# A two-layer cross-attention kernel on one core: first-layer norms as one operation per tile, norm weights applied on leaving PSUM

## The chip, the cores and the metric

The kernel runs on one core of a Trainium2 chip. A core has five engines, each with its own instruction queue: TensorE (PE, matrix products), VectorE (DVE), ScalarE (ACT), GpSimd (POOL) and SyncE (SP, which here only starts transfers). They meet through semaphores. The metric is the device time of one execution in microseconds; less is better.

## What is computed

Two cross-attention layers over 2 batches of 512 tokens of width 256, with a context of 1024 rows of width 192. Layer 0 (which the program counts as −1, and which the change touches) has one head, layer norms on both inputs, and biases:

```python
qn = _layer_norm(q_feat, g_q, be_q)          # (x - mu) * rsqrt(var + EPS) * gamma + beta
kvn = _layer_norm(kv_feat, g_kv, be_kv)
q = einsum('bnq,eq->bne', qn, Wq) + bq
k = einsum('bmk,ek->bme', kvn, Wk) + bk
v = einsum('bmk,ek->bme', kvn, Wv) + bv
attn = softmax(einsum('bne,bme->bnm', q, k), axis=-1)
x = q_feat + einsum('bnf,ef->bne', einsum('bnm,bme->bnf', attn, v), Wd) + bd
...
# layer 1: 8 heads of 256, keys and values from the raw context, mask; out = LayerNorm(ctx @ Wo + x)
```

## The kernel before

Every fp32 operand of a large product is split into a rounded high part and a low remainder, and a product is made of three passes (`three`, line 569) or of five for scores and values. ACT writes the high parts (`round_...`), DVE or POOL the low parts (`split_...`). Wq and Wk, and Wv and Wd, are first multiplied with each other (`absorb`), so that queries meet the normalised context directly. The weights come through two buffers, `ring`, as pieces.

The order of each engine's work is written out by hand, in one long list per engine: SP lines 325 to 422, POOL 426 to 564, PE 568 to 980, ACT 984 to 1332, DVE 1336 to 1789. An instruction that waits holds everything behind it on its engine.

Layer 0 in the order of PE (lines 788 to 867): a product of spread biases with the weights (792); transposes of the normalised tokens, chunks 0 and 1 (`turn_chunk`, `xn`); weight products (`absorb`); small bias products (803); transposes of the normalised context, chunks 2 to 5 (`kvn`); `queries` for batch 0; then `scores(-1, j)` for blocks of 128 queries, j = 0 to 3, each into the same two PSUM banks `ps_scores`, which DVE's `minimum` (1352) must have read before the next block may write. ACT's `exp`, PE's `turn_probs`, ACT's `round_probs` and DVE's `split_probs` follow for each block, and `values` for the batch; batch 1's norms run between these.

A norm takes, for one tile: statistics and moments on DVE (`ln_stats`, `ln_moments`), a power of −1/2 on POOL (`rsqrt`), centring and the weight on DVE (`ln_centre`), scaling on ACT (`scale_tiles`), the bias on POOL (`bias_tiles`); for half of the context tiles scaling and bias are one operation on DVE (`ln_scale_context`). Every score is shifted by a query-dependent number, which DVE sums from the normalised tokens (`sum_shift`, `finish_shift`) ahead of the first minimum of a batch.

## Time and profile before

| | us |
|---|---|
| median of 3 runs | 501.74 (501.72 to 502.06) |
| profiled execution | 501.67 |
| its span, first to last instruction | 499.70 |
| PE busy in the span | 474.2 |
| DVE / ACT / POOL busy | 332.2 / 291.6 / 245.4 |

The span is what the trace covers; the profiled execution's own time is 1.97 us longer. A row of the timeline gives start, duration, engine, line, operation, output and inputs, the number of merged instructions (x4), and in brackets how long the engine was idle before it and what released it. PE's ends are modelled: two rows that follow each other overlap by their latency, so the time of one in a sequence is read from start to start. A product of plain fp32 operands shows as two instructions.

### The profile page before, as it was taken

What the parts mean: (1) busy time and instruction counts of PE and PEld (TensorE: products, weight loads), DVE (VectorE), ACT (ScalarE), POOL (GpSimd) and SP (SyncE); (2) the same over time, 40 slices, a digit from 0 to 9 for tenths busy, and PEclk for the clock granted to TensorE, in tenths of its full rate; (3) what the DMA queues carried; (4) which work ended last, traced back from release to release, by engine and by line L of the source; (5) the groups of instructions that cost most, each with busy time, mean ns of one, the idle gap of its engine ahead of it and who ended that gap; (6) DMA issues with size and microseconds to landing.
All of it is one profiled execution on the core that took longest, in us unless ns stands there. A gap on an engine that the chain in (4) does not pass through costs nothing.

```text
span 499.7 us, 7565 instructions
## 1 busy us (share of the span) xinstructions
PE 474.2 (95%) x2424; PEld 395.8 (79%) x2424; DVE 332.2 (66%) x679; ACT 291.6 (58%) x482; POOL 245.4 (49%) x153
## 2 busy tenths in 40 slices
PE   0999999999999999999999999999999999999994
PEld 0877787787878888888888888888888888888893
DVE  4999866476685657565856585658565765673666
ACT  4667476467664756566666665656565655556332
POOL 4636763555855353637272717172727263454004
PEclk9999999999999999999999999999999999999998
DMA  8413013667765565665656564647473746562002
GB/s 263 147 45 127 1 29 120 212 206 227 246 214 182 177 202 176 205 211 168 210 168 210 168 214 164 226 153 238 140 244 135 252 137 220 168 210 64 0 2 84
DMA packets 53975, 81.97 MB, mean 164 GB/s; under 512 B 5793, under 2 KB 43073, under 8 KB 53825
## 3 DMA queue, kind: packets, MB, share of 16 engines
q1 hardware_dynamic: 44992, 50.16, 33.8%
q10 hardware_dynamic: 8960, 31.54, 16.8%
q8 instruction: 11, 0.18, 0.2%
q14 instruction: 12, 0.09, 0.1%
HBM read 49.16 MB, written 32.51 MB: 163 GB/s over the span
## 4 chain that ended last, share of the span: by engine, by line
PE 74%; DVE 8%; DMA 7%; ACT 4%; issue 3%; POOL 2%; SPq 1%; DVEq 0%; POOLq 0%; ACTq 0%
PE ps_scores L626 27%; PE ps_o L658 6%; PE ps_o L651 5%; PE ps_o L650 5%; PE ps_o L657 5%; PE ps_o L652 5%; DMA scratch<-probs 3%; PE ps_task L574 2%; PE ps_task L573 2%; PE ps_task L572 2%; DMA probs_t_lo<-scratch 2%; DMA ring<-in_weights_a 2%; PE ps_out L572 2%; PE ps_out L573 1%; PE ps_out L574 1%
## 5 line engine op out<-in xcount | busy, mean ns | idle before, releaser
L514 POOL TENSOR_TENSOR probs_t_lo<-probs_t_lo,probs_t_hi 128x1024 fp32r<-128x1024 f32 (+1 forms) x75 | 146.5, 1967 | 177.5 <-ACT probs_t_hi L1018 177.4
L1018 ACT ACTIVATE probs_t_hi<-probs_t_lo 128x1024 fp32r<-128x1024 f32 (+1 forms) x75 | 64.7, 881 | 37.2 <-DMA probs_t_lo<-scratch 34.7
L626 PE MATMUL ps_scores<-key_hi,q_hi 128*128 128x512 f32 x144 | 57.8, 402 | 1.3 <-DVE neg_scores L1352 0.8
L1339 DVE RECIPROCAL row_inv<-row_sum 128x1 f32<-128x1 f32 x72 | 11.3, 159 | 70.4 <-PE ps_scores L626 68.4
L650 PE MATMUL ps_o<-probs_t_hi,val_hi 128*128 128x512 f32 (+1 forms) x144 | 56.7, 393 | 1.1 <-issue 0.9
L626 PE MATMUL ps_scores<-key_rem,q_lo 128*128 128x512 f32 x144 | 56.6, 393 | 0.5 <-DVE q_lo L1434 0.3
L626 PE MATMUL ps_scores<-key_rem,q_hi 128*128 128x512 f32 x144 | 56.6, 393 | 0.0
L626 PE MATMUL ps_scores<-key_lo,q_hi 128*128 128x512 f32 x144 | 56.6, 393 | 0.0
L626 PE MATMUL ps_scores<-key_hi,q_lo 128*128 128x512 f32 x144 | 56.4, 392 | 0.0
L651 PE MATMUL ps_o<-probs_t_lo,val_hi 128*128 128x512 f32 (+1 forms) x144 | 56.3, 391 | 0.0
L658 PE MATMUL ps_o<-probs_t_lo,val_rem 128*128 128x512 f32 (+1 forms) x144 | 56.2, 392 | 0.0
L657 PE MATMUL ps_o<-probs_t_hi,val_rem 128*128 128x512 f32 (+1 forms) x144 | 55.8, 389 | 0.0
L652 PE MATMUL ps_o<-probs_t_hi,val_lo 128*128 128x512 f32 (+1 forms) x144 | 55.6, 386 | 0.0
L1376 DVE STREAM_TRANSPOSE probs<-probs 128x1024 f32<-128x1024 f32 x30 | 37.4, 1246 | 25.0 <-ACT probs L1006 24.8
L1376 DVE STREAM_TRANSPOSE neg_scores<-neg_scores 128x1024 f32<-128x1024 f32 x30 | 37.3, 1242 | 15.1 <-ACT neg_scores L1006 15.1
L444 POOL TENSOR_TENSOR w_lo<-ring,w_hi 128x1024 fp32r<-128x1024 f32 x17 | 40.9, 2408 | 6.2 <-ACT w_hi L1098 6.2
L1006 ACT ACTIVATE neg_scores<-neg_scores,row_min 128x1024 f32<-128x1024 f32 x30 | 34.5, 1148 | 13.1 <-DVE row_min L1369 13.1
L1369 DVE CUSTOM_DVE_ANT_0 probs<-ps_scores,mask_bias 128x1024 f32<-128x1024 f32 x32 | 38.9, 1216 | 3.2 <-PE ps_scores L626 3.2
L1006 ACT ACTIVATE probs<-probs,row_min 128x1024 f32<-128x1024 f32 x30 | 34.5, 1151 | 11.1 <-DVE row_min L1369 11.0
L1369 DVE CUSTOM_DVE_ANT_0 neg_scores<-ps_scores,mask_bias 128x1024 f32<-128x1024 f32 x32 | 38.8, 1213 | 0.6 <-issue 0.6
L626 PEld LDWEIGHTS ps_scores<-key_hi,q_hi 128*128 128x128 f32 x144 | 27.0, 188 | 7.5 <-DVE neg_scores L1352 2.2
L626 PEld LDWEIGHTS ps_scores<-key_rem,q_lo 128*128 128x128 f32 x144 | 27.0, 188 | 7.2 <-DVE q_lo L1434 0.6
(256 smaller groups left out, 1097.5 us busy)
## 6 DMA issues: line engine op xcount, KB each, us to landing
probs_t_lo<-scratch SPq DMA_DIRECT2D x240, 128.0 KB, 2.9
scratch<-neg_scores ACTq DMA_DIRECT2D x30, 512.0 KB, 3.1
scratch<-probs ACTq DMA_DIRECT2D x30, 512.0 KB, 3.7
ring<-in_weights_a SPq DMA_DIRECT2D x9, 512.0 KB, 5.2
ring<-in_weights_b SPq DMA_DIRECT2D x9, 512.0 KB, 5.1
ring<-in_keys_t SPq DMA_DIRECT2D x4, 512.0 KB, 3.2
ctx_raw<-in_context SPq DMA_DIRECT2D x2, 768.0 KB, 9.5
ring<-in_context SPq DMA_DIRECT2D x16, 96.0 KB, 2.6
```

Of the source, the lines that this page charges most:

```text
L444: nc.gpsimd.tensor_tensor(w_lo[:, :], ring[r][:, :], w_hi[:, :].bitcast(f32), ALU.subtract)\
L514: nc.gpsimd.tensor_tensor(pt_lo[b][:, t, k, :], pt_lo[b][:, t, k, :].bitcast(f32), moved_part(j, k).bitcast(f32), ALU.subtract).then_inc(m ...
L626: last = pe.matmul(ps_scores[:, n], left, right[:, n], start=(i == 0), stop=(i == len(passes) - 1))
L650: pe.matmul(o0, val_hi[b][:, kt, :], hi, start=(kt == 0), stop=False)
L651: pe.matmul(l0, val_hi[b][:, kt, :], lo, start=False, stop=False)
L652: pe.matmul(o0, val_lo[b][:, kt, :], hi, start=False, stop=(kt == KT - 1))
L657: pe.matmul(o1, val_rem[b][:, kt, :], hi, start=(kt == 0), stop=False)
L658: last = pe.matmul(l1, val_rem[b][:, kt, :], lo, start=False, stop=(kt == KT - 1))
L1006: act.activation(dst, src, ACT.Exp, bias=row_min[:, j:j + 1], scale=-1.0, accum_out=row_sum[:, j:j + 1]).then_inc(exped, 1)
L1018: act.activation(moved_part(j, k), pt_lo[b][:, t, k, :].bitcast(f32), ACT.Copy)\
L1369: dve.tensor_tensor_reduce(out=tiles[j % 2][:, :], in0=ps_scores[:, :], in1=mask_bias[:, b, :], scale=1.0, scalar=BIG, op0=ALU.add, op1=AL ...
L1376: dve.transpose(tiles[j % 2][:, :], tiles[j % 2][:, :]).then_inc(blocks_turned, 1)
```

## The change

One norm operation per tile: ACT makes (x · r − m · r) from the raw tile for tokens and half of the context (`norm_tokens`, `norm_context` on ACT), DVE makes (x − m) · r for the other context tiles (`norm_context` on DVE). For ACT's form DVE first makes −m · r (`shift_means`), which needs POOL's r. The norm weights are multiplied in when ACT and DVE take transposed chunks (`round_chunk`, `split_chunk`) and the output weights (`round_b`, `split_b0`) out of PSUM; for that the weights come as one row on one partition (`gain_row`) and PE turns them into columns (`gains`). The norm biases are folded into the projection biases by reductions over the weights (`fold_bias`). The score shift is made on PE, from a split vector of two columns and the split tokens (`sum_shift`), kept by ACT (`keep_shift`), turned back by PE (`turn_shift`) and finished on DVE. PE multiplies the identity with itself 20 times ahead of the first chunks and 8 times ahead of the weight products (`keep_running`); nothing reads the result. Tokens, context rows and outputs are assigned to partitions in stretches that lie together in memory. Transfers, and the second weight piece's rounding on ACT, change places. The core of the diff (the lines not shown are declarations, the same edits for the context and the outputs, and `split_w` and `fold_bias`, which follow below it):

```diff
-    x_tiles = x.rearrange("(t p) d -> p t d", p=P)
+    x_tiles = x.rearrange("(b p t) d -> b p t d", p=P, t=QT)
...
 @block.sync
+            sp.dma_start(resid[:, 0:QT, :], x_tiles[0]).then_inc(x_loaded[0], 16)
+            sp.dma_start(ctx_raw[:, 0:CTX_HALF, :], ctx_tiles[0, :, 0:CTX_HALF, :]).then_inc(ctx_loaded[0], 16)
+            sp.dma_start(ctx_raw[:, CTX_HALF:KT, :], ctx_tiles[0, :, CTX_HALF:KT, :]).then_inc(ctx_loaded[1], 16)
             sp.dma_start(ring[0][:, :], weights_a[0]).then_inc(ring_loaded[0], 16)
+            sp.dma_start(be_row[:, :], rows_q[1].partition_broadcast(P)).then_inc(be_row_loaded, 16)
+            sp.dma_start(kv_row[:, :], rows_kv[1].partition_broadcast(P)).then_inc(kv_row_loaded, 16)
             sp.dma_start(ring[1][:, :], weights_b[0]).then_inc(ring_loaded[1], 16)
...
 @block.tensor
-                    pe.wait_ge(task_free, T_VEC + 1)
+                    pe.wait_ge(chunk_split, 1)
...
+            def keep_running(count):
+                for i in range(count):
+                    pe.matmul(ps_scores[:, BANK:BANK + P], ident[:, :], ident[:, :], start=True, stop=True)
+            def sum_shift(b, bank):
+                for k in range(DT):
+                    mv = slice(b * QUERIES, (b + 1) * QUERIES)
+                    pe.matmul(bank[0:2, :], w_pair[:, k, :], xt_hi[:, k, mv], start=(k == 0), stop=False)
+                    last = pe.matmul(bank[0:2, :], w_pair[:, k, :], xt_lo[:, k, mv], start=False, stop=(k == DT - 1))
+                last.then_inc(shift_rowed, 1)
+            def turn_shift(b, bank):
+                pe.wait_ge(shift_kept, b + 1)
+                if b == 0:
+                    for k in range(DT):
+                        pe.matmul(bank[:, V_CONST:V_CONST + 1], ones[:, :], shift_parts[:, k:k + 1],
+                                  start=(k == 0), stop=(k == DT - 1))
+                for t in range(QT):
+                    last = pe.transpose(bank[:, 2 * t:2 * t + 2], shift_rows[:, t, :], ident[0:2, 0:2])
+                last.then_inc(shift_turned, 1)
...
-            pe.wait_ge(spread_made, DT)
-            pe.wait_ge(ring_loaded[0], 16)
-            raw = ring[0]
-            for k in range(DT):
-                pe.matmul(vec_bank[:, DIM:2 * DIM], spread[:, k, :], raw[:, k * DIM:(k + 1) * DIM],
-                          start=(k == 0), stop=(k == DT - 1))
             pe.wait_ge(ident_loaded, 16)
-            for c in range(X_CHUNKS):
+            pe.wait_ge(gain_row_loaded, 48)
+            for n in range(N_GAINS):
+                last = pe.transpose(vec_bank[:, V_GAINS + n:V_GAINS + n + 1], gain_row[:, n * P:(n + 1) * P],
+                                    ident[0:1, 0:1])
+            last.then_inc(gains_turned, 1)
+            keep_running(20)
+            for c in range(X_CHUNKS + 1):
                 turn_chunk(0, c)
+            keep_running(8)
             pe.wait_ge(piece_split, PC_A0 + 1)
             absorb(T_A0, 0)
             absorb(T_A0b, 1)
+            for c in range(X_CHUNKS + 1, CHUNKS):
+                turn_chunk(0, c)
+            pe.wait_ge(bias_folded, 2)
...
-            for c in range(X_CHUNKS, CHUNKS):
-                turn_chunk(0, c)
             pe.wait_ge(chunk_split, X_CHUNKS)
+            pe.wait_ge(w_split, 1)
+            sum_shift(0, w_bank)
             pe.wait_ge(task_free, T_VEC + 1)
             queries(T_Q0, 0, 0)
             queries(T_Q0b, 0, 1)
-            pe.wait_ge(chunk_split, CHUNKS)
+            turn_shift(0, w_bank)
+            pe.wait_ge(chunk_split, CHUNKS - 2)
...
             for c in range(QT):
                 values(-1, 0, c)
+                if c == 0:
+                    pe.wait_ge(task_free, T_Q1 + 1)
+                    sum_shift(1, ps_task)
+                if c == 1:
+                    turn_shift(1, ps_task)
...
 @block.scalar
+            act.dma_start(ident[:, :], identity).then_inc(ident_loaded, 16)
+            act.dma_start(gain_row[:, 0:DIM], rows_q[0:1]).then_inc(gain_row_loaded, 16)
+            act.dma_start(gain_row[:, DIM:DIM + CTX], rows_kv[0:1]).then_inc(gain_row_loaded, 16)
+            act.dma_start(gain_row[:, DIM + CTX:2 * DIM], rows_kv[0:1, P:CTX]).then_inc(gain_row_loaded, 16)
             act.dma_start(cols[:, :], vectors).then_inc(cols_loaded, 16)
-            act.dma_start(ident[:, :], identity).then_inc(ident_loaded, 16)
...
+            def norm_tokens(b):
+                act.wait_ge(means_made, 2 * b + 1)
+                for t in range(KT, LN_TILES):
+                    n, x_tile = b * LN_TILES + t, b * QT + t - KT
+                    act.activation(xn[:, x_tile, :], resid[:, x_tile, :], ACT.Identity,
+                                   scale=rstd[:, n:n + 1], bias=neg_means[:, n:n + 1]).then_inc(x_normed, 1)
...
-                act.activation(dst, chunk_bank(b, c)[:, 0:BANK], ACT.Copy).then_inc(chunk_rounded, 1)
+                act.activation(dst, chunk_bank(b, c)[:, 0:BANK], ACT.Copy, scale=scale).then_inc(chunk_rounded, 1)
...
-            round_weights(16, 1)
+            keep_shift(0, w_bank)
             act.wait_ge(vec_made, 1)
             round_queries(T_Q0, 0, 0, 0)
             round_queries(T_Q0b, 0, 1, 0)
+            round_weights(16, 1)
+            act.wait_ge(bias_v_folded, 1)
+            for k in range(DT):
+                act.activation(spread[:, DT + k, :], ones[:, :], ACT.Copy, scale=bias_cols[:, C_BV + k:C_BV + k + 1])\
+                    .then_inc(spread_made, 1)
             exp(-1, 0)
...
 @block.vector
+            def norm_context(b):
+                dve.wait_ge(rstd_made, 3 * b + 3)
+                for t in range(CTX_HALF, KT):
+                    n = b * LN_TILES + t
+                    dve.tensor_scalar(kvn[b][:, t, 0:CTX], ctx_raw[:, b * KT + t, :], moments[:, n, 0:1],
+                                      rstd[:, n:n + 1], ALU.subtract, ALU.mult).then_inc(ctx_normed[1], 1)
+            def shift_means(b, first, end, rstds):
+                n = slice(b * LN_TILES + first, b * LN_TILES + end)
+                dve.wait_ge(rstd_made, 3 * b + rstds)
+                dve.scalar_tensor_tensor(neg_means[:, n], moments[:, n, 0], -1.0, rstd[:, n], ALU.mult, ALU.mult)\
+                    .then_inc(means_made, 1)
...
             ln_stats(0, x_token_tiles, x_loaded[0])
             ln_moments(0, KT, LN_TILES)
-            dve.wait_ge(q_rows_loaded, 16)
-            ln_centre(0, x_token_tiles)
-            ln_stats(0, range(KT), ctx_loaded[0])
-            ln_moments(0, 0, KT)
+            ln_stats(0, range(CTX_HALF), ctx_loaded[0])
+            ln_moments(0, 0, CTX_HALF)
+            shift_means(0, KT, LN_TILES, 1)
+            shift_means(0, 0, CTX_HALF, 2)
...
+            ln_stats(0, range(CTX_HALF, KT), ctx_loaded[1])
+            ln_moments(0, CTX_HALF, KT)
+            norm_context(0)
             dve.wait_ge(piece_hi, HI_OF[PC_A0])
...
             split_queries(T_Q0, 0, 0, 0)
             split_queries(T_Q0b, 0, 1, 0)
-            sum_shift(0, range(QT))
-            finish_shift(0)
+            split_chunk(0, 4)
+            split_chunk(0, 5)
+            finish_shift(0, w_bank[:, 0:2 * QT])
+            dve.wait_ge(ring_loaded[1], 16)
+            fold_bias(C_BV, ring[1], 0, kv_row, bias_v_folded)
             minimum(-1, 0, 0)
             ln_stats(1, x_token_tiles, x_loaded[1])
             ln_moments(1, KT, LN_TILES)
+            shift_means(1, KT, LN_TILES, 1)
             split_b0(T_B0, 0)
             split_b0(T_B0b, 1)
```

```python
def fold_bias(side, raw, first, row, folded_by):
    for k in range(DT):
        dve.tensor_tensor_reduce(out=probs[...], in0=raw[...], in1=row[:, :], op0=ALU.mult, op1=ALU.add,
                                 accum_out=bias_parts[:, side + k:side + k + 1]).then_inc(bias_summed, 1)
    dve.wait_ge(bias_summed, side + DT)
    dve.tensor_tensor(bias_cols[:, n], bias_parts[:, n], cols[:, n], ALU.add).then_inc(folded_by, 1)
def split_w():
    dve.tensor_copy(w_pair[:, :, 0], made).then_inc(w_hi_made, 1)
    dve.tensor_tensor(shift_parts[:, 0:DT], bias_cols[...], bias_cols[...], ALU.mult)
    dve.wait_ge(w_hi_made, 1)
    dve.tensor_tensor(w_pair[:, :, 1], made, w_pair[:, :, 0], ALU.subtract).then_inc(w_split, 1)
```

## Rows read from the trace of the kernel before

**Rows 1.** The page's first part: engines, busy us, share of the span, instructions.

```profile
PE 474.2 (95%) x2424; PEld 395.8 (79%) x2424; DVE 332.2 (66%) x679; ACT 291.6 (58%) x482; POOL 245.4 (49%) x153
```

**Rows 2.** Stretches: length; PE, PEld, DVE, ACT, POOL busy us; granted clock; DMA share; GB/s.

```profile
33.00:46.80 13.80, 11.94 (x65) 9.27 (x65) 12.96 (x33) 12.39 (x23) 8.81 (x7) 1.00 0.41 153
46.80:59.05 12.25, 11.76 (x56) 8.98 (x56) 12.04 (x34) 4.89 (x12) 10.94 (x13) 1.00 0.00 1
...
200.00:249.00 49.00, 49.00 (x245) 41.22 (x244) 31.83 (x60) 29.70 (x46) 24.25 (x12) 1.00 0.62 201
```

**Rows 3.** Timeline of the head, DVE, POOL and ACT, 4 to 14 us.

```profile
4.72 1.41 DVE L1470 BATCH_NORM_STATS2 stats<-resid 128x6 f32<-128x256 f32 x4 [4.72 <-DMA resid<-in_x]
...
6.77 1.02 POOL L431 TENSOR_TENSOR rstd<-var_eps,minus_half 128x4 f32<-128x4 f32 x1 [4.63 <-DVE var_eps L1481]
...
7.82 1.71 ACT L1127 ACTIVATE xn<-xn,rstd 128x256 f32<-128x256 f32 x4 [1.16 <-POOL rstd L431]
...
9.84 2.17 DVE L1470 BATCH_NORM_STATS2 stats<-ctx_raw 128x6 f32<-128x192 f32 x8 [1.15 <-DMA ctx_raw<-in_context]
11.65 1.06 ACT L1098 ACTIVATE w_hi<-ring 128x1024 fp32r<-128x1024 f32 x1 [2.12 <-DMA ring<-in_weights_a]
...
12.74 1.23 DVE L1556 TENSOR_TENSOR w_lo<-ring,w_hi 128x1024 fp32r<-128x1024 f32 x1
```

**Rows 4.** Timeline of PE alone, 11 to 40 us.

```profile
11.76 2.04 PE L792 MATMUL ps_o<-ring,b_full 128*128 128x256 f32 x4 [11.76 <-DMA ring<-in_weights_a]
13.60 1.91 PE L779 MATMUL ps_turn<-ident,xn 128*128 128x128 f32 x8
...
16.59 0.41 PE L572 MATMUL ps_out<-w_hi 128*128 128x256 f32 x1
...
16.99 0.28 PE L574 MATMUL ps_out<-w_hi,w_lo 128*128 128x256 f32 x1
...
17.46 0.95 PE L803 MATMUL ps_o<-cols,ring 128*128 128x1 f32 x8
...
23.53 0.39 PE L574 MATMUL ps_task<-xt_hi,a_lo 128*128 128x512 f32 x1
...
31.84 1.03 PE L827 MATMUL ps_out<-ring,b_full 128*128 128x256 f32 x4
...
39.52 1.04 PE L779 MATMUL ps_o<-ident,xn 128*128 128x128 f32 x8
```

**Rows 5.** Timeline of all engines from the last query products to the third score block.

```profile
22.95 2.39 POOL L444 TENSOR_TENSOR w_lo<-ring,w_hi 128x1024 fp32r<-128x1024 f32 x1 [2.93 <-ACT w_hi L1098]
...
24.68 0.74 DVE L1434 SCALAR_TENSOR_TENSOR q_lo<-ps_task,vec,q_hi 64x512 fp32r<-64x512 f32 x1 [0.36 <-ACT q_hi L1075]
...
27.20 1.28 DVE L1352 TENSOR_SCALAR_CACHE_REDUCE neg_scores<-ps_scores,neg_shift 128x1024 f32<-128x1024 f32 x1
...
28.54 0.50 PE L626 MATMUL ps_scores<-key_hi,q_hi 128*128 128x512 f32 x1
...
30.37 1.02 POOL L431 TENSOR_TENSOR rstd<-var_eps,minus_half 128x4 f32<-128x4 f32 x1 [5.03 <-DVE var_eps L1481]
...
31.67 1.28 DVE L1352 TENSOR_SCALAR_CACHE_REDUCE neg_scores<-ps_scores,neg_shift 128x1024 f32<-128x1024 f32 x1
...
33.02 0.50 PE L626 MATMUL ps_scores<-key_hi,q_hi 128*128 128x512 f32 x1 [0.16 <-DVE neg_scores L1352]
```

**Rows 6.** DMA issues of the first 30 us: KB each, us from issue to landing.

```profile
cols<-in_vectors ACTq DMA_DIRECT2D x1, 3.0 KB, 3.3
mask_bias<-in_mask ACTq DMA_DIRECT2D x1, 8.0 KB, 6.9
```

**Rows 7.** DVE's groups by line and shape, 27.2 to 59.05 us: busy us, mean ns.

```profile
L1501 DVE SCALAR_TENSOR_TENSOR kvn<-kvn,rstd,kv_rows 128x192 f32<-128x192 f32 x4 | 3.0, 799 | 0.0
L1492 DVE SCALAR_TENSOR_TENSOR kvn<-ctx_raw,moments,kv_rows 128x192 f32<-128x192 f32 x8 | 2.7, 412 | 0.0
...
L1529 DVE CUSTOM_DVE_ANT_0 ctx_raw<-xn,rem_sum 128x256 f32<-128x256 f32 x4 | 1.4, 409 | 0.0
```

More of the change, by code:

```diff
@@ L415, in store @@
                 sp.wait_ge(fin_made[half], count)
[L416 removed]
+                sp.dma_start(out_tiles[b, :, t, :], tiles[:, t, :])\
                     .then_inc(stored, 16)
@@ L623, in scores @@
                                 pe.wait_ge(task_free, task + (1 if i == 2 else 2))
+                        if late_keys is not None and half == 1 and i in (0, 3):
+                            pe.wait_ge(chunk_split, late_keys + (1 if i == 0 else 2))
                         if keys is not None and i == 3 and half == 0:
@@ new lines, in shift_means @@
+            def shift_means(b, first, end, rstds):
[4 more added lines that the diff above has]
+            def fold_bias(side, raw, first, row, folded_by):
+                n = slice(side, side + DT)
+                width = row.shape[1]
+                for k in range(DT):
+                    spare, src = side % (2 * DT) * DIM + k * width, first + k * DIM
+                    dve.tensor_tensor_reduce(
+                        out=probs[:, spare:spare + width], in0=raw[:, src:src + width], in1=row[:, :], scale=1.0, scalar=0.0, op0=ALU.mult, op1=ALU.add,
+                        accum_out=bias_parts[:, side + k:side + k + 1]).then_inc(bias_summed, 1)
+                dve.wait_ge(bias_summed, side + DT)
+                dve.tensor_tensor(bias_cols[:, n], bias_parts[:, n], cols[:, n], ALU.add).then_inc(folded_by, 1)
```

248 lines of the change are left out of this document (127 added, 121 removed).

## Prediction

> **What bounds the kernel now.** I read the page's busy shares first: TensorE (PE) is busy 95% of the span, no other engine above 79% [rows 1]. Then the stretches: from 200 to 249 us, which stands for the long middle, PE is busy 49.00 of 49.00 us, so nothing that shortens another engine's work there can shorten the kernel; the change touches nothing there. Its edits all lie before about 60 us, and there PE has holes: 13.80 − 11.94 = 1.86 us in 33.0 to 46.8, 12.25 − 11.76 = 0.49 us in 46.8 to 59.05 [rows 2]. VectorE (DVE) is busy 12.96 of 13.80 and 12.04 of 12.25 us in the last two, so it, in a chain with PE and ScalarE (ACT), ends those holes. Third, the timeline of the head: PE does nothing before 11.76 us, when the first weights land [rows 4]. So a delay or a gain that stands on PE at 60 us is carried to the end unchanged, and the task is to find where PE stands there. The sum is made against the profiled execution, 501.67 us (span 499.70 and 1.97 around it); the median of three is 501.74, the same within 0.07.
>
> I use two marks of before. T is the end of the first query products: the last starts at 23.53 and is followed 0.23 us later, so T = 23.76 [rows 4]. The second mark is the start of the third score block, 33.02 [rows 5].
>
> **Part 1, the head up to T.** Removed: the two 256-column products with spread biases (11.76 to 13.60, the start of the first transposes, 1.84 us), GpSimd's (POOL) bias additions, DVE's centring. Added on PE: four tiny transposes of the gains, 20 idle products, 8 more, two extra bias products, four products for the score shift.
>
> When PE starts: it now waits for the identity and three gain rows on ACT's queue. The third gain row is issued after three others, at about 0.73 + 3 × 0.5 = 2.2 us. The biases, first on that queue, took 3.3 us to land, the mask, third, 6.9 [rows 6]; so the start is 5.5 us by the one and 9.1 by the other, and not before the tokens that move at the same time, 4.7 [rows 3]. I take 5.5: the queue's big transfer, the identity, now goes first and beside the tokens. The Trainium skill (DMA: Bandwidth & Descriptors, "Queues, rings and completion order") says that an engine serves the queues in turn, packet by packet, and in "Anatomy of one DMA" it puts the fixed cost near 2 us; by that the start would be an estimated 4.2 us, the low part of the weights would decide, and the sum would be 504.7. The mask's 6.9 us speaks against it, the biases' 3.3 us for it in part.
>
> An idle product is 128 columns of fp32 and issues two instructions. The two 256-column products at 11.76 make four instructions in 1.84 us, so a 128-column one costs 0.46 us at that clock; the same pair at 31.84 takes 1.03, so a half-size one about 0.23 to 0.26 [rows 4]. The clock: 256-column instructions last 0.41 us at 16.59 and 0.28 at 16.99, the step from 1.2 to 2.4 GHz, 5.1 us after PE began. If PE begins at 5.5, the step comes at 10.6. Gains to 6.1; ten idle products to 10.6 at 0.45; ten more at 0.23 to 12.9; twelve transposes (eight take 1.04 at 39.52 including the last one's tail, so 0.115 each) to 14.3; eight idle products to 16.1. The idle products keep PE warm, but the last ones stand in its queue ahead of the weight products.
>
> Are the inputs there by 16.1? Tokens land at 4.72, their reciprocal deviation is ready at 6.77 + 1.02 = 7.79 [rows 3]. From token landing to the first weights (11.65), 1.77 MB came in 6.9 us; at that rate half the context lands at 6.3, all of it at 7.8 and the weights, with 0.45 MB fewer ahead, at 9.9. Statistics of four context tiles (2.17 / 8 each) and moments end at 8.2, POOL's power at 9.3, DVE's mean shift, which waits for it, at 9.6; behind that wait stand the second half's statistics, which then end at 11.3, POOL at 12.4, four normalising operations (at most the 2.7 / 8 of a centring each [rows 7]) at 13.8, the weights' low part (1.23) at 15.0. ACT normalises tokens 8.4 to 10.1 (1.71), four context tiles to 11.6, rounds the weights (1.06) to 12.7. So the low part is ready at 15.0, against 13.97 before, and PE's own queue at 16.1 decides. Weight products: twelve at 0.12 (16.99 to 17.46 holds four) end at 17.5, where before they ended at 17.46. The whole gain in clock is spent on idle products.
>
> From there to T before: 6.3 us. After: twelve transposes, 1.4; sixteen bias instructions at 0.95 / 8, 1.9; then PE waits for DVE to copy, split and subtract the small vector (three short operations, 0.15 to 0.2 each: 0.6); four shift products at 0.23, 0.9; twelve query products, 2.8. T comes at 25.1, **1.3 us later**. Ends: +0.5 with a start at 4.7, +4.9 with 9.1 (every us of start is a us of T, until the low part at 15.0 decides).
>
> **Part 2, T to the third score block.** Two queues grow. ACT now rounds the second weight piece after both query halves (T + 0.8 to T + 1.9), and POOL splits it in 2.39 [rows 5]: T + 4.35, then twelve products, and the second score block starts at T + 5.8; before it was 28.54 = T + 4.8. DVE, after the second query split (24.68 + 0.74 = T + 1.66), has two more key splits (0.7 each), the shift's finish (three short ones, 0.5) and the value-bias fold (two reductions of about 0.35 and an addition, 0.8; the removed reductions took 0.41 each [rows 7]), so the first minimum starts at T + 4.4 instead of T + 3.44: **+0.95**. ACT's first exponential also waits for that fold, but the minimum is later.
>
> Then the wait that the change adds: after batch 1's token moments DVE's mean shift waits for POOL's power of the variances just made. Row 30.37 has this power at 1.02 us [rows 5]; with two hand-overs and the operation itself 1.3 us. Behind it on DVE stand the two output-weight splits, the mask steps and the second minimum. Before, minimum to minimum was 31.67 − 27.20 = 4.47; now 5.8, so the second starts at T + 10.2 against T + 7.91: **+2.25 in all**, the 0.95 included. The third score block needs the bank that this minimum empties, and starts that much later. PE's second block ends near T + 8.2 and cannot hide it.
>
> **Part 3, to 59 us.** DVE loses the token centring ahead of the third minimum, 2.7 and 3.0 us of context work and 1.4 of shift sums [rows 7], some 7 us; it gains about 2 us of new work. What is that worth? At most the 1.86 us of holes. But scores and minimum alternate on one pair of banks: after the lift the third minimum waits for its scores instead of the centring. I take 0.35 us of the 1.86 (bounds 0.3 and 1.9), since ACT's order between the third block and the value products is unchanged. In batch 1 PE gets four shift products (0.9) and four transposes (0.5) between value products; the 0.49 us of holes there go. **+0.9.** ACT waits for the shift rows ahead of four context tiles, 3 us before PE asks for these. The plain-scale multiplications on leaving PSUM cost nothing more on ACT, and up to 0.06 us each on DVE, hidden. Contiguous memory: at most 0.3 us of the last store, taken as 0.
>
> **Sum:** 1.3 + 2.25 − 0.35 + 0.9 = +4.1, so 501.67 + 4.1 = 505.8 us.
>
> **Rivals.** First, *faster by DVE's relief*: DVE is the engine without pause after 33 us, and about 7 us go. If POOL's power is out of the way when DVE needs it and the extra operations before the minima fit beside PE, then all holes go (−2.49), the shift costs 1.4, the head is even (start 4.7 and low part at 14.5), the store gives 0.2: 500.4. It decides if the second minimum starts by T + 8. For it: DVE's 12.96 of 13.80; against it: program order, which puts the wait ahead of the minimum. Chance 0.13.
>
> Second, *about even*: the clock steps up early, or the head is 1.3 us shorter than I have it (T at 23.8) and the power trip costs half: 0 + 1.6 − 1.5 + 0.9 = +1.0, 502.7 or a little below. Chance 0.14.
>
> Third, *gain rows late*: PE starts at 9.1, T + 4.9, total 509.4. For it: the mask's 6.9 us; against: what lay ahead of the mask. Chance 0.08.
>
> That the change does not do what it says: the idle products may not lift the clock before the weight products (they are 128 columns, as the transposes in before are): then the 28 cost 12.6 us instead of 8.6 and T is 4 us later still, near 510; this lies within the third's chance.
>
> **How the numbers follow.** My forecast has 0.65: 503.5 (start 4.7, holes worth 1.9) to 507.5 (start 7.2). The range takes in the even case and most of the way to the late one, and leaves out the faster case and the end of the late one, 0.19 in all: 501.5 to 508.5. Faster and slower mean by over 0.2% (1.0 us), about what a measurement of this kernel can tell from no change: faster 0.13, same 0.14, slower 0.73.
>
> **What would show it.** Right: PE idle products from about 5.5 to 13 and eight more ending near 16; first 0.28 us weight product at once; T near 25; a DVE idle of about 1.2 us put down to POOL's power between first and second minimum; third score block at 36.5 to 37.5; 200 to 249 unchanged. Wrong: a start of PE before 4.5 or after 8; weight products before 14.5 (then the inputs were earlier than I have them); the second minimum within 8 us of T; PE's holes from 33 to 47 gone.

## The result, and the profile after

The changed kernel takes 508.58 us (median of 4, 508.48 to 508.86), the kernel before beside it 501.90: a ratio of 1.0135, 95% interval 1.0119 to 1.0151. The forecast was 505.8, range 501.5 to 508.5: the direction was right, the size too small, and the time lies just outside the range. The profiled execution took 508.56, of which 506.4 are the span. Two single executions in the experiments, 792.49 us (the kernel before with the added wait) and 1228.55 us (the kernel with six edits, in the execution that was profiled), are left out of every median here.

The page of the changed kernel, engines as in [rows 1]:

```profile
PE 484.6 (96%) x2504; PEld 405.2 (80%) x2504; DVE 326.5 (64%) x666; ACT 295.8 (58%) x483; POOL 231.9 (46%) x139
```

PE has 10.4 us more work, mostly idle products; DVE and POOL have 5.7 and 13.5 us less. From 200 to 249 us (columns as in [rows 2]) PE is busy 49.00 of 49.00 us in both kernels, so what was lost was lost early:

```profile
200.00:249.00 49.00, 49.00 (x246) 41.19 (x245) 31.84 (x59) 29.78 (x47) 24.26 (x12) 1.00 0.59 193
```

The timeline of PE in the head, to be held against [rows 4]:

```profile
6.47 0.56 PE L829 MATMUL ps_o<-ident,neg_scores 1*128 1x1 f32 x4 [6.47 <-DMA neg_scores<-in_rows_kv]
6.95 6.97 PE L799 MATMUL ps_scores<-ident 128*128 128x128 f32 x40
13.76 1.04 PE L793 MATMUL ps_turn<-ident,xn 128*128 128x128 f32 x8
...
15.07 1.95 PE L799 MATMUL ps_scores<-ident 128*128 128x128 f32 x16
16.78 0.36 PE L584 MATMUL ps_task<-w_hi 128*128 128x256 f32 x1
...
19.60 0.95 PE L847 MATMUL ps_o<-bias_cols,ring 128*128 128x1 f32 x8
20.41 1.03 PE L851 MATMUL ps_o<-bias_cols,ring 128*128 128x1 f32 x8
22.05 0.59 PE L805 MATMUL ps_turn<-xt_hi,w_pair 128*2 128x512 f32 x1 [0.61 <-DVE w_pair L1594]
22.43 0.63 PE L806 MATMUL ps_turn<-xt_lo,w_pair 128*2 128x512 f32 x1
22.86 0.63 PE L805 MATMUL ps_turn<-xt_hi,w_pair 128*2 128x512 f32 x1
...
27.01 0.40 PE L586 MATMUL ps_task<-xt_hi,a_lo 128*128 128x512 f32 x1
```

The last query product starts at 27.01 and is followed 0.24 us later, so T is 27.25 against 23.76. The shift products at 22.43 and 22.86 are 0.43 us apart, those around 27 us 0.23. The stretches of the same profile say why (length; PE, PEld, DVE, ACT, POOL busy; granted clock; DMA share; GB/s):

```profile
19.60:22.05 2.45, 1.84 (x19) 1.79 (x17) 0.57 (x5) 1.17 (x3) 0.00 (x0) 0.97 0.00 0
22.05:25.00 2.95, 2.95 (x8) 1.65 (x9) 1.28 (x2) 0.59 (x1) 0.00 (x0) 0.50 0.55 178
25.00:27.25 2.25, 2.25 (x11) 1.83 (x10) 0.41 (x1) 0.69 (x1) 0.00 (x0) 0.92 0.00 0
```

PE did 1.84 us of one-column products, then waited 0.61 us for DVE; from there the granted clock is 0.50, the lower level (1.2 GHz), for about 3 us. Sixteen products took 27.25 − 22.05 = 5.20 us; at 0.23 each they take 3.7. The fall costs 1.5 us.

From T to the third score block, all engines, against [rows 5]:

```profile
29.16 2.38 POOL L460 TENSOR_TENSOR w_lo<-ring,w_hi 128x1024 fp32r<-128x1024 f32 x1 [17.28 <-ACT w_hi L1157]
...
30.86 0.90 DVE L1582 CUSTOM_DVE_ANT_0 probs<-ring,kv_row 128x192 f32<-128x192 f32 x1
...
32.19 1.28 DVE L1429 TENSOR_SCALAR_CACHE_REDUCE neg_scores<-ps_scores,neg_shift 128x1024 f32<-128x1024 f32 x1
...
35.36 1.01 POOL L455 TENSOR_TENSOR rstd<-var_eps,minus_half 128x4 f32<-128x4 f32 x1 [3.82 <-DVE var_eps L1559]
36.40 0.16 DVE L1573 SCALAR_TENSOR_TENSOR neg_means<-moments,rstd 128x4 f32<-128x4 f32 x1 [1.12 <-POOL rstd L455]
...
38.08 1.28 DVE L1429 TENSOR_SCALAR_CACHE_REDUCE neg_scores<-ps_scores,neg_shift 128x1024 f32<-128x1024 f32 x1
...
39.43 0.50 PE L640 MATMUL ps_scores<-key_hi,q_hi 128*128 128x512 f32 x1 [1.28 <-DVE neg_scores L1429]
```

The first minimum starts at T + 4.94 (before T + 3.44), the second at T + 10.83 (T + 7.91), the third block at T + 12.18 (T + 9.26): 2.92 us later against T, and the added wait stands there as forecast, 1.12 us of DVE's idle time put down to POOL's power. From the third to the fourth block both kernels take 4.08 us. Then the stretch from the fourth to the fifth block, first before, then after:

```profile
37.10:59.05 21.95, 20.26 (x102) 15.53 (x102) 20.89 (x56) 13.24 (x27) 17.50 (x17) 1.00 0.19 73
```

```profile
43.51:66.72 23.21, 21.44 (x111) 16.20 (x111) 18.03 (x43) 14.93 (x28) 13.67 (x13) 1.00 0.19 69
```

It is 1.26 us longer: PE has 1.18 us more work, and its idle time is 1.69 us before and 1.77 after, though DVE has 2.86 us less to do. At the fifth block the changed kernel is 3.49 + 2.92 + 1.26 = 7.67 us behind. From about 165 to 196 us it gets 0.93 back: there the profiled execution before has small waits for DVE (the largest, 0.41 us, at 195.43) and the changed one none:

```profile
195.43 0.38 PE L572 MATMUL ps_out<-b_hi,o_hi 128*128 128x256 f32 x1 [0.41 <-DVE b_lo L1448]
```

With that, 6.7 us arrive at the end of the span.

### The profile page after: what moved, and what is told of

It reads as the page before. It is cut to its first block, busy times and chain, and to the rows that moved or that the text cites. A ratio compares the mean times of both kernels' runs of the same rounds, so it can differ in the third digit from the quotient of the medians.

```text
span 506.4 us, 7697 instructions
## 1 busy us (share of the span) xinstructions
PE 484.6 (96%) x2504; PEld 405.2 (80%) x2504; DVE 326.5 (64%) x666; ACT 295.8 (58%) x483; POOL 231.9 (46%) x139
## 3 DMA queue, kind: packets, MB, share of 16 engines
q10 hardware_dynamic: 8966, 31.54, 16.5%
## 4 chain that ended last, share of the span: by engine, by line
PE 86%; DVE 5%; ACT 4%; issue 1%; POOL 1%; DMA 1%; ACTq 0%; DVEq 0%; POOLq 0%
PE ps_scores L640 29%; PE ps_o L664 7%; PE ps_o L672 7%; PE ps_o L665 7%; PE ps_o L671 6%; PE ps_o L666 6%; PE ps_task L586 3%; PE ps_task L585 3%; PE ps_task L584 3%; PE ps_out L584 2%; PE ps_scores L799 2%; PE ps_out L585 2%; PE ps_out L586 2%; PE ps_out L758 1%; PE ps_out L757 1%
## 5 line engine op out<-in xcount | busy, mean ns | idle before, releaser
L640 PEld LDWEIGHTS ps_scores<-key_rem,q_hi 128*128 128x128 f32 x144 | 27.0, 188 | 6.8 <-ACT q_hi L1132 0.4
```

The source lines that it names most:

```text
L640: last = pe.matmul(ps_scores[:, n], left, right[:, n], start=(i == 0), stop=(i == len(passes) - 1))
```

## Experiments

Times are medians; the kernel before took 501.3 to 501.8 beside them, and "less" and "more" are against the changed kernel's 508.58 unless another is named. T is always the end of the first query products.

**Why the clock fell.** First, the bias products ahead of chunks 3 to 5, so that the transposes cover DVE's split:

```diff
-            for c in range(X_CHUNKS + 1, CHUNKS):
-                turn_chunk(0, c)
             pe.wait_ge(bias_folded, 2)
...
             last.then_inc(task_done, 1)
+            for c in range(X_CHUNKS + 1, CHUNKS):
+                turn_chunk(0, c)
             pe.wait_ge(chunk_split, X_CHUNKS)
```

> The changed kernel with its 16 one-column bias products ahead of the transposes of chunks 3 to 5 instead of behind them; nothing left out. In the changed kernel PE waits 0.61 us for VectorE's split of the small vector, the granted clock falls from 0.97 to 0.50 and the next eight products are 0.42 us apart instead of 0.23. Theory (the one-column products directly followed by the wait let the clock fall): the transposes cover the split, the wait goes, the clock stays up, the first query products end 2.1 us earlier (0.6 wait, 1.5 clock) and so does everything behind them: 506.4, or 507 if some of it is given back between 165 and 196 us. Rival (the one-column products alone let the clock fall, whatever stands behind them): the transposes then run at half clock, 1.3 us longer, only the wait goes; 508 to 508.5.

505.78 us, 2.80 less. T is 24.43: 0.6 of the gain is the wait, 1.5 the clock, and 0.57 comes from the head, where the weight products started at 16.21 in this execution. PE's timeline: no wait, and products at the upper clock (0.24 us apart from the second on).

```profile
18.54 1.03 PE L848 MATMUL ps_o<-bias_cols,ring 128*128 128x1 f32 x8
...
20.70 0.47 PE L805 MATMUL ps_turn<-xt_hi,w_pair 128*2 128x512 f32 x1
21.01 0.40 PE L806 MATMUL ps_turn<-xt_lo,w_pair 128*2 128x512 f32 x1
21.25 0.39 PE L805 MATMUL ps_turn<-xt_hi,w_pair 128*2 128x512 f32 x1
```

The one-column products alone do not bring the clock down. Second, the changed kernel's own order with the wait filled:

```diff
+            pe.wait_ge(task_free, T_VEC)
+            for i in range(3):
+                pe.matmul(ps_out[:, 0:P], ident[:, :], ident[:, :], start=True, stop=True)
             pe.wait_ge(chunk_split, X_CHUNKS)
```

> The changed kernel, in its own order, with three idle products (0.7 us at full clock) put into the 0.61-us wait between the one-column bias products and the shift products; nothing left out. This tells the two causes of the fallen clock apart that the run with the bias products first couldn't. Theory (the wait behind the one-column products brings the clock down): with the wait filled the granted clock stays at its upper level, the shift and query products are 0.23 us apart, the first query products end 1.4 to 1.5 us sooner; 507.1. Rival (the 1.8 us of one-column products bring it down alone): the products behind are still 0.42 us apart, the idle ones also slow; 508.6 to 509.4.

506.84 us, 1.74 less, though no useful work was moved. The stretches of the idle products and of the sixteen products behind them:

```profile
20.82:21.56 0.74, 0.74 (x8) 0.74 (x8) 0.56 (x5) 0.00 (x0) 0.00 (x0) 1.00 0.00 0
21.56:25.24 3.68, 3.68 (x18) 2.70 (x17) 1.67 (x3) 1.28 (x2) 0.00 (x0) 1.00 0.39 142
```

Sixteen products in 3.68 us at a granted clock of 1.00, against 5.20: filling 0.6 us of waiting gives 1.5 us back. (T is 25.24, 2.01 sooner; the other 0.48 is again the head, where the weight products started at 16.30.) In all eight executions of these two runs the mean granted clock of the whole span is 0.995 or 0.996; in the four of the changed kernel it is 0.993 or 0.994.

**The idle products.** The eight behind the first transposes left out:

```diff
-            keep_running(8)
```

> The changed kernel without the eight idle products between the first transposes and the weight products; nothing left out. In the changed kernel those eight end at 16.78 us and the low part of the weights is there at 14.30. Theory (they stand in the queue ahead of work that is ready): the weight products start at 15.1 at full clock, the first query products end 1.6 to 1.7 us sooner, the clock still falls behind the one-column products; 506.9 to 507.2. Rival (the eight keep the clock up for the weight products): these start 0.21 us apart, end 0.6 us sooner at most; 508 or above.

506.41 us, 2.17 less. The weight products start at 15.16 instead of 16.78: the eight were only in the way. The profiled execution (505.32 us, the fastest of the four) shows one thing more: the wait is there, and the clock stayed up.

```profile
20.44 0.40 PE L805 MATMUL ps_turn<-xt_hi,w_pair 128*2 128x512 f32 x1 [0.61 <-DVE w_pair L1593]
20.68 0.39 PE L806 MATMUL ps_turn<-xt_lo,w_pair 128*2 128x512 f32 x1
```

So one-column products and a wait of 0.6 us do not always lose the clock. Of the seven profiles with this wait four show the fall (the changed kernel, without idle products, mean shift late, the queues; 5.19 to 5.27 us for the sixteen products) and three don't (without the eight, start early, batch 1's shift moved; 3.66 to 3.69); of the five without the wait none does (3.64 to 3.73). Within one kernel it shows in the times: with the mean shift moved (below), 505.55 us where the mean granted clock was 0.996, and 507.48 to 507.73 where it was 0.992. The Trainium skill (TensorE: Matmul & The Clock Gate, "What's actually happening") says of the step upward that "it's run-variable"; these runs show the same of the fall. What no run here tells is whether a wait of 0.6 us behind full-width products would lose the clock too; in the kernel before with an added wait (below) PE waits 1.00 us for POOL behind transposes, and the 512-column products behind it are 0.23 us apart, the distance of the upper clock.

PE started early, with twelve idle products on the tile of ones ahead of the wait for the gain rows:

```diff
+            pe.wait_ge(ones_set, 1)
+            for i in range(12):
+                pe.matmul(ps_scores[:, BANK:BANK + P], ones[:, :], ones[:, :], start=True, stop=True)
             pe.wait_ge(ident_loaded, 16)
```

> The changed kernel with 12 more idle products, on the tile of ones, ahead of its wait for the identity and the gain rows, so that PE runs from about 1 us instead of 6.47; nothing left out. This prices the step of the prediction that had PE start at 5.5 us and counted a microsecond of start as a microsecond of the first query products. Theory: the clock steps up near 6 us, the 20 idle products take 4.6 us instead of 6.8, the first transposes end near 13, the eight idle ones near 14.9, the weight products start near 15.0 instead of 16.78 and all that follows comes 1.7 us sooner: 506.8, with the clock falling as before behind the one-column products. Rival (the start doesn't count, the inputs of the transposes or the weights' low part hold PE): under 0.5 us, 508.1 or above.

504.64 us, 3.94 less. The 20 idle products take 4.6 us, and the weight products start 2.47 us sooner, now at the moment at which their low part is ready:

```profile
6.40 4.73 PE L799 MATMUL ps_scores<-ident 128*128 128x128 f32 x40
...
14.31 0.39 PE L584 MATMUL ps_task<-w_hi 128*128 128x256 f32 x1
```

The clock stayed up here as well (T at 23.30), which is the rest of the 3.94. What PE gets rid of ahead of the weight products counts one for one, as the prediction had it, until their low part decides. But it is the idle products that got shorter (6.8 us in the changed kernel): the gain rows landed at 6.09 here, and no run moves their landing by itself. Without any idle products:

```diff
-            keep_running(20)
...
-            keep_running(8)
```

> The changed kernel without its 28 idle products; nothing that is computed is left out. In the changed kernel the weight products start at 16.78 us at full clock (0.12 us apart), though the low part of the weights is ready at 14.30, so the idle products cost 2.4 us of waiting and buy the clock. Theory (the idle products pay for themselves): without them the weight products start at 14.3 but at half clock, twelve at 0.21 us end near 16.9 instead of 18.3, and the 12 transposes, 16 one-column products, 4 shift products and 12 query products that follow also run at half clock, so that the first query products end at 28 to 29 us instead of 27.25: 509 to 510.5 us in all. Rival (idle products are only a delay): the clock is up soon after the first weight product, the first query products end 2 us earlier and the time is 506 to 507.

509.23 us (508.73 to 509.58), 0.65 more, but not as expected: T is at 26.37, 0.9 sooner. PE runs only the first twelve transposes (10.16 to 13.0), waits 1.34 us for the low part of the weights, and the weight products are 0.21 us apart, the distance of the lower clock:

```profile
14.38 0.58 PE L584 MATMUL ps_task<-w_hi 128*128 128x256 f32 x1 [1.34 <-DVE w_lo L1646]
14.76 0.41 PE L585 MATMUL ps_task<-w_lo,w_hi 128*128 128x256 f32 x1
14.97 0.41 PE L586 MATMUL ps_task<-w_hi,w_lo 128*128 128x256 f32 x1
```

(The column of the granted clock reads 1.00 from 14.38 to 17.11 all the same; the kernel before reads 1.00 from 14 to 16 us too, where its products of 256 columns are 0.21 us apart. In the head the level has to be read from the distances.) The 0.9 us and more are lost again later: near 88 us PE waits 1.84 us for ACT (0.75 in the changed kernel), which had waited 0.97 for a transfer, and near 225 us 0.72 for DVE. Neither account fits: in the head of this kernel the idle products cost 0.9 us more than they bring, and why the kernel without them waits more later stays open.

**The two minima.** The mean shift behind the second minimum instead of ahead of it:

```diff
-            shift_means(1, KT, LN_TILES, 1)
...
             minimum(-1, 1, 0)
+            shift_means(1, KT, LN_TILES, 1)
```

> The changed kernel with VectorE's mean shift of batch 1's tokens moved from ahead of the second minimum to behind it; nothing left out. There VectorE idles 1.12 us on GpSimd's power of the variances. Theory (the wait stands on the chain): the second minimum starts 1.2 to 1.3 us sooner, the third score block too, and the time is 507.3 (507.8 if part is given back at 165 to 196 us). Rival (the bank is not what the third block waits for, or ScalarE behind the minimum sets the pace): the third block keeps its place and the time stays within 0.3 us of 508.6.

507.57 us, 1.01 less; T is 27.70, and the third block starts at T + 11.06, 1.12 sooner. The wait was on the chain.

```profile
38.76 0.50 PE L640 MATMUL ps_scores<-key_hi,q_hi 128*128 128x512 f32 x1 [0.46 <-DVE neg_scores L1429]
```

And the wait alone, put into the kernel before:

```diff
             ln_moments(1, KT, LN_TILES)
+            dve.wait_ge(rstd_made, 3)
```

> The kernel before with one wait added and nothing else: behind batch 1's token moments VectorE waits until GpSimd's power of these variances is done, as the changed kernel's mean shift makes it. This prices by itself the wait that the prediction put at 1.3 us. Theory: the moments end near 30.4 us, the power at 31.4, the output-weight splits, the mask steps and the second minimum start 1.1 to 1.3 us later, the third score block too: 502.4 to 502.7 against 501.3. Rival (the second minimum waits for its scores or for ScalarE anyway): not over 0.3 us, 501.6.

502.43 us (median of nine), a ratio of 1.0021 to the kernel before (1.0007 to 1.0036), 1.1 us more. T is 23.95, and the third block starts at T + 10.50, 1.24 later than in the kernel before:

```profile
31.62 0.42 DVE L1423 TENSOR_TENSOR b_lo<-ps_out,b_hi 128x256 fp32r<-128x256 f32 x1 [1.13 <-POOL rstd L431]
...
33.10 1.28 DVE L1352 TENSOR_SCALAR_CACHE_REDUCE neg_scores<-ps_scores,neg_shift 128x1024 f32<-128x1024 f32 x1
...
34.45 0.50 PE L626 MATMUL ps_scores<-key_hi,q_hi 128*128 128x512 f32 x1 [1.22 <-DVE neg_scores L1352]
```

Up to the third block the wait costs 1.24 us where it is added and gives 1.12 where it is taken out. Then the two queues, ACT's step first, DVE's two behind it:

```diff
+            round_weights(16, 1)
             keep_shift(0, w_bank)
...
             round_queries(T_Q0b, 0, 1, 0)
-            round_weights(16, 1)
...
+            dve.wait_ge(ring_loaded[1], 16)
+            fold_bias(C_BV, ring[1], 0, kv_row, bias_v_folded)
             dve.wait_ge(task_done, T_VEC + 1)
...
+            split_chunk(0, 4)
+            split_chunk(0, 5)
             split_queries(T_Q0, 0, 0, 0)
             split_queries(T_Q0b, 0, 1, 0)
-            split_chunk(0, 4)
-            split_chunk(0, 5)
             finish_shift(0, w_bank[:, 0:2 * QT])
-            dve.wait_ge(ring_loaded[1], 16)
-            fold_bias(C_BV, ring[1], 0, kv_row, bias_v_folded)
```

> The changed kernel with the order of three steps altered on their engines, nothing left out: ScalarE rounds the second weight piece ahead of keeping the shift, where it idles 3.2 us, instead of behind both query halves; VectorE folds the value biases ahead of its wait for the small vector, where it idles 2.2 us; and it splits the last two key chunks ahead of the query halves, where it idles 3.5 us. Theory (the two queues behind the first query products delay the first minimum and the second score block): the second score block starts 0.5 us sooner against the first, the first minimum 2 to 2.4 us sooner, the third block 1.5 to 2 us sooner; the time is 506.6 to 507.1, or 0.5 above that if part is given back later. Rival (PE's own order of work sets the third block): not over 0.5 us, 508.1 or above.

506.88 us, 1.70 less. The second block follows the first by 4.00 us (5.53 in the changed kernel), the first minimum starts at T + 3.41, where it waits for scores, and the third block 1.54 us sooner against T. (What each of the three moves gives alone was not run.) The fold's first reduction takes 0.35 us at its new place:

```profile
18.71 0.35 DVE L1582 CUSTOM_DVE_ANT_0 probs<-ring,kv_row 128x192 f32<-128x192 f32 x1
...
30.11 1.28 DVE L1429 TENSOR_SCALAR_CACHE_REDUCE neg_scores<-ps_scores,neg_shift 128x1024 f32<-128x1024 f32 x1 [1.29 <-PE ps_scores L640]
```

**Batch 1.** The four shift products moved behind the first query half, into a bank that is free there (ACT's `keep_shift` moves with them):

```diff
             queries(T_Q1, 1, 0, chunks=True)
+            sum_shift(1, ps_o[0])
...
+            pe.wait_ge(shift_kept, 2)
...
-                    sum_shift(1, ps_task)
```

> The changed kernel with batch 1's four shift products moved to where PE idles 0.51 us on VectorE, in a bank that is free there, and nothing else; nothing left out. This prices the shift of batch 1 alone, where the changed kernel's third to fourth stage is 1.26 us longer. Theory (four products of 0.23 and the transposes, 1.2 us of PE's time, and no relief from VectorE): of 0.9 us of products 0.4 to 0.6 go into the idle time; 508.0 to 508.2. Rival (VectorE's and ScalarE's normalising of the context makes that stage longer, not the products): no change, 508.5 or more.

506.19 us (505.73 to 508.85). The clock did not fall in the profiled execution (T at 25.48), so the total can't be compared; the stage can:

```profile
41.77:64.63 22.86, 21.38 (x110) 16.18 (x110) 17.93 (x43) 14.74 (x28) 13.66 (x13) 1.00 0.18 70
```

22.86 against 23.21: 0.35 of the 0.9 us of products went into idle time. What is left of the longer stage is PE's own added work: 21.38 us against 20.26 before, with 1.48 idle against 1.69. The one execution of the four at 508.85 us has a mean granted clock of 0.991, as where the clock falls, and shows no gain over 508.58; so the 0.35 us is shown in the stage and not in the total.

**All together.** The four diffs above in one: the bias products first, the mean shift late, the queues, and no eight idle products:

> The changed kernel with four edits together: bias products ahead of the transposes, mean shift behind the second minimum, three steps moved into idle time of ScalarE and VectorE, and no eight idle products; nothing left out. Alone the first three gave 2.8, 1.0 and 1.7 us. Theory (these losses lie one behind the other on one chain): they add, with 1.6 for the eight idle products, to 7.1 us, and the time is 501.5, level with the kernel before; what stays lost is 1.3 us in batch 1, what is gained is the relief of VectorE. Rival (they hide one another, or a later transfer sets the pace once the head is short): 503 to 504.5.

501.64 us, ratio to the kernel before 1.0006 (0.9996 to 1.0016): the four gains nearly add up, 6.94 us together where the single ones sum to 7.68, and T is at 23.06, ahead of before. This profile also tells what the relief of DVE is worth once the wait is gone: the third block starts at 32.61 (33.02 before), the fourth 4.09 us later (4.08 before), and the stretch from the fourth to the fifth is as long as in the changed kernel, with 1.70 us idle on PE:

```profile
36.70:59.87 23.17, 21.47 (x111) 16.20 (x111) 18.05 (x43) 14.95 (x28) 13.66 (x13) 1.00 0.18 69
```

With batch 1's shift products moved as above, and the mask steps ahead of the first minimum:

```diff
+            dve.wait_ge(mask_loaded, 16)
+            dve.tensor_scalar(mask_small, mask_small.bitcast(i32), 0.0, BIG, ALU.is_equal, ALU.mult)...
+            dve.tensor_scalar(mask_small, mask_small, 10.0, None, ALU.mult)...
             minimum(-1, 0, 0)
```

> The kernel of the four edits (501.64 us) with two more; nothing left out. The mask steps stand ahead of the first minimum, where VectorE idles 1.3 us on scores, instead of ahead of the second; batch 1's four shift products stand between the query halves and the last transposes, where PE idles 0.49 us on VectorE, in a bank that is free there, instead of between value products. Theory (both were on the chain): the second minimum starts 0.4 us sooner, and 0.6 of the 1.2 us that batch 1 lost comes back: 500.5 us, 0.8 below the kernel before (501.3). Rival (the next wait, VectorE's or ScalarE's, takes each place): 501.4 to 501.7.

500.97 us (median of twelve), ratio 0.9990 (0.9977 to 1.0003). By the medians it is 0.7 better than four edits, though the two intervals overlap, and ahead of the kernel before by no more than the measurement can tell. Which of the two edits gives what, no profile shows. The same two kernels without the first 20 idle products (`keep_running(20)` left out), first with four edits, then with six:

> The kernel of the four edits (501.64 us) without its first 20 idle products, so with none; nothing left out. With the other losses gone this prices the idle products. Theory (they pay now): the weight products start at 14.5 as before but 0.21 us apart, end 1.1 us later, the one-column and shift products follow later by that, 502.6 to 503.2. Rival (VectorE's split of the small vector, near 19.2 us, decides and not PE): the shift products start where they did and the time stays within 0.4 us of 501.6.

504.24 us, from 502.23 to 506.54. In the profiled execution (502.23) the products behind the 1.34-us wait are 0.12 us apart without any idle product, in the next kernel's 0.21:

```profile
14.32 0.38 PE L584 MATMUL ps_task<-w_hi 128*128 128x256 f32 x1 [1.34 <-DVE w_lo L1645]
14.54 0.28 PE L585 MATMUL ps_task<-w_lo,w_hi 128*128 128x256 f32 x1
14.66 0.28 PE L586 MATMUL ps_task<-w_hi,w_lo 128*128 128x256 f32 x1
```

> The kernel with the six edits (500.99 us) without its first 20 idle products; nothing left out. With four edits this gave 502.2 to 506.5 us, too wide to tell. Theory (without idle products it is left to chance when the clock is up, and this shows as scatter of more than 1 us from run to run): times between 501 and 504, the median over 501.5. Rival (the clock comes up by itself before the weight products, as the profiled run of that kernel showed): 500.8 to 501.2, no scatter.

506.36 us, from 502.51 to 508.68. Without idle products it is left to chance when the clock is up. T is 22.81 in the one profile and 23.93 in the other, which explains about 1 us of the scatter; the second profile also has a wait of 1.39 us at 220.8 us and one of 0.68 at 197.0, both for DVE, that the profile of the four edits has not. Why kernels without idle products at the start should meet more of these stays open.

**Parts of the change alone, in the kernel before.** Twenty-eight idle products on ones at its start:

```diff
+            pe.wait_ge(ones_set, 1)
+            for i in range(28):
+                pe.matmul(ps_scores[:, BANK:BANK + P], ones[:, :], ones[:, :], start=True, stop=True)
             pe.wait_ge(spread_made, DT)
```

> The kernel before with 28 idle products on the tile of ones at its start, from about 1 us to about 11 us, and nothing else: the part of the change that keeps PE running, alone. Theory (a warm clock shortens PE's own head but the inputs set the end): the bias products and first transposes end at 13.7 instead of 15.2 us, the weight products run at 0.12 us apart from 14.1 and end near 15.6 instead of 17.46; the fifth chunk of transposes still waits for the normalised context that GpSimd hands over near 19.8, so the query products end at most 0.3 us sooner and the time is 501.5 to 501.8, no change. Rival (PE's head is the chain): 1.8 us sooner, 500.0.

500.93 us against 501.32, ratio 1.0000 (0.9983 to 1.0017). PE ran to 9.79, then waited 1.98 us for the weights, and the clock fell again; from 12.76 on it is 0.50:

```profile
9.79:11.77 1.98, 0.01 (x2) 0.03 (x1) 1.98 (x9) 0.11 (x1) 1.47 (x3) 1.00 1.02 404
12.76:16.00 3.24, 3.24 (x17) 3.24 (x16) 3.24 (x8) 1.89 (x5) 1.71 (x2) 0.50 1.08 332
```

Behind its twelve one-column products PE then waits 1.32 us for DVE, and the clock falls a second time:

```profile
19.33:22.57 3.24, 3.24 (x17) 3.24 (x17) 3.21 (x8) 2.31 (x5) 0.00 (x0) 0.52 0.38 138
```

T is 25.56 in this execution (502.51 us, the third slowest of the ten), 1.8 later than before. No change, as expected, though in part for another reason: in this execution two falls of the clock take the gain back. And tokens and outputs in contiguous stretches:

```diff
-    x_tiles = x.rearrange("(t p) d -> p t d", p=P)
+    x_tiles = x.rearrange("(b p t) d -> b p t d", p=P, t=QT)
-    out_tiles = out.rearrange("(t p) d -> p t d", p=P)
+    out_tiles = out.rearrange("(b p t) d -> b p t d", p=P, t=QT)
...
```

> The kernel before with tokens and outputs in contiguous stretches of memory (each partition's four rows of a batch beside one another) and nothing else: the change's layout alone, without that of the context. Theory (it hides): the tokens land up to 0.4 us sooner and the context decides the head as before; the last stores are up to 0.3 us shorter; 501.0 to 501.3, no change. Rival (the longer stretches free the queues for what follows): context and weights land 1 us sooner too, 500.3.

501.11 us, ratio 0.9994 (0.9979 to 1.0008). Tokens landed at 4.18 instead of 4.72, and the first weights no sooner (11.97): it hides.

## Why the prediction was right or wrong

| step | forecast | measured |
|---|---|---|
| T, PE's start and idle queue | +1.3 | +1.97 |
| T, granted clock falls | 0 | +1.52 |
| first minimum against T | +0.95 | +1.50 |
| mean shift's wait, up to the third block | +1.3 | +1.42 |
| holes from DVE's relief | −0.35 | 0 |
| batch 1 on PE | +0.9 | +1.26 |
| given back in the second layer | 0 | −0.93 |
| sum | +4.1 | +6.7 |

What bounds the kernel was right: the early stages decide, and each microsecond there reached the end but for 0.93 us. The prediction has no term for this; that the time lies only 0.1 us beyond its range is owed to it, and is luck. The start was mis-sized: the gain rows landed at 6.47, not 5.5, between the two bounds and nearer the lower one, so the rival of late gain rows (9.1) did not come about; nor did idle products that don't lift the clock, for the weight products behind them are 0.12 us apart. The 4.2 us that the prediction worked out from the Trainium skill (DMA: Bandwidth & Descriptors, "Anatomy of one DMA") came 2.3 us too early, and the measurement decides: that section gives its fixed cost near 2 us for transfers issued from GpSimd, while the gain rows stand on ACT's queue. That PE's own queue and not the low part of the weights (ready at 14.30) decides was right: the runs without the eight and with the early start show it.

The step that failed is the one at the end of Part 1, "then PE waits for DVE ...: 0.6; four shift products at 0.23, 0.9; twelve query products, 2.8". The wait came as written (0.61), but all sixteen products were costed at the upper clock. The prediction asked only whether the idle products would lift the clock, never what the new work behind them, 1.84 us of one-column products and then a wait, would do to it. In the kernel before, the transposes of chunks 2 to 5 stand between the one-column products and the query products; the first two runs show that this cover is worth the wait and 1.5 us of clock.

In Part 2 mechanism and place were right, and the wait was sized rightly (1.3 forecast; 1.12 and 1.24 up to the third block in two runs). The fold was too cheap: 0.90 us for its first reduction instead of 0.35, which is all of the step from +0.95 to +1.50. It starts beside POOL's weight split, which runs from 29.16 to 31.54, and ends just after it, at 31.7; moved ahead of the vector, where POOL is idle, it took 0.35. The Trainium skill (GPSIMD Engine Reference, "8. Key points") says that GpSimd shares its SBUF interfaces with VectorE and contends with VectorE instructions that have two SBUF inputs; this reduction has two, and the two durations agree with that.

In Part 3 the relief of DVE was taken at 0.35 and was worth nothing: the third block waits for the second minimum and then the two alternate, 4.08 us in both. That the shift products cost PE 0.9 was right; the transposes (0.5) were set off against 0.49 us of holes, and these holes did not go: PE has 1.18 us more work in the stage and its idle time went from 1.69 to 1.77. That scaling costs ACT nothing more as it takes a chunk out of PSUM was wrong as well (about 0.69 us a chunk against 0.60), though no wait of PE here is put down to it. The rival that needed DVE's relief fails by its own condition in the changed kernel (second minimum at T + 10.83, not by T + 8), and the kernel with four edits, where the added wait is gone and the second minimum starts at T + 8.20, keeps 4.09 us and 1.70 us of idle time all the same.

## What to carry to other kernels

Idle products are worth their place only if they run up to the moment at which the next inputs are ready, and no further; count the ones behind that as delay. When the clock has to be kept up, look for every place where tiny products stand just ahead of a wait: put work that has to be done anyway between these products and the wait for what another engine makes of them, or fill the wait. And a smaller sum of operations on an engine gives nothing while program order puts one wait for another engine ahead of the operation that frees the bank.

## What the runs showed of the hardware

A wait of 0.6 us behind 1.84 us of one-column products was enough for the granted clock to fall to 0.50 in four profiles of seven; with the wait filled or covered it fell in none of five. In one of the four (mean shift late) the first two products behind the wait still ran 0.22 us apart, and the fall came after them.

In the kernel before with idle products the clock fell behind a wait of 1.98 us that followed 8.8 us of full-width products, about 0.9 us after PE had begun again, and once more behind 1.39 us of one-column products and a wait of 1.32 us.

A reduction over two SBUF tensors of 192 columns took 0.90 us where it started beside a POOL operation, and 0.35 without one. POOL's power of 128x4 numbers took 1.01 to 1.02 us and kept the waiting DVE idle for 1.06 to 1.13.
